# Causal mask of a diagonal score tile: two products with 128 columns of weights for eight with 32

## What is computed

```
scores = einsum('bhqd,bhkd->bhqk', q, k)           # 16 heads of 8 features, 2048 x 2048
scores = where(causal, scores, -inf)
attn   = softmax(scores / sqrt(8), axis=-1)
ctx    = einsum('bhqk,bhkd->bhqd', attn, v)
```

## Time and profile before

| | |
|---|---|
| median of 3 runs | 1156.01 us (1155.78 to 1160.44) |
| the profiled execution's own time | 1162.2 us |
| its span | 1160.4 us |
| PE busy | 1054.0 us (91%), 14718 products |
| VectorE busy | 972.7 us (84%) |
| ScalarE busy | 661.3 us (57%) |
| L1985 products | 2048, mean 222 ns |
| attention layers | about 185 to 572 and 751 to 1134 us |

### The profile page before, as it was taken

The page is one execution under the profiler, slowest core; times in us unless marked ns, Lnnn a source line. Parts: engine busy times, 40 slices in busy tenths (PEclk is TensorE's granted clock), DMA queues, the critical chain, the costliest instruction groups (busy, mean ns, idle before and its releaser), DMA issues.

```text
span 1160.4 us, 34497 instructions
## 1 busy us (share of the span) xinstructions
PE 1054.0 (91%) x14718; PEld 483.9 (42%) x14718; DVE 972.7 (84%) x2307; ACT 661.3 (57%) x852; POOL 100.6 (9%) x124
## 2 busy tenths in 40 slices
PE   4989968999999999999998857799999999999998
PEld 2545543333333333334557826333333333333446
DVE  7787579999999999988544866899999999998854
ACT  3322214566787778777523222246667777777784
POOL 1431010000000000000042252000000000000000
PEclk9999999999999999999998979799999999999999
DMA  5061052000000000000001032220000000000001
GB/s 166 2 255 72 28 163 67 3 2 3 2 2 2 3 3 3 2 3 3 2 30 46 29 91 82 74 57 3 2 3 3 2 3 2 3 2 3 3 3 38
DMA packets 29493, 36.68 MB, mean 32 GB/s; under 512 B 3694, under 2 KB 26388, under 8 KB 29084
## 3 DMA queue, kind: packets, MB, share of 16 engines
q1 hardware_dynamic: 27228, 29.22, 7.6%
q0 software_dynamic: 2112, 5.25, 1.7%
HBM read 15.29 MB, written 18.87 MB: 29 GB/s over the span
## 4 chain that ended last, share of the span: by engine, by line
PE 51%; DVE 38%; issue 5%; ACT 4%; DMA 1%; another core or an unknown queue 1%; POOL 0%; SPq 0%; DVEq 0%; ACTq 0%; POOLq 0%
DVE part_max L2174 28%; PE psum L1999 12%; PE psum L2020 11%; PE psum L1970 6%; PE psum L520 5%; PE psum L1648 2%; PE psum L1985 2%; ACT hidden L2113 2%; PE psum L2053 1%; PE psum L2026 1%; DVE xn L204 1%; PE psum L299 1%; PE psum L544 1%; PE psum L1247 1%; PE psum L1259 1%
## 5 line engine op out<-in xcount | busy, mean ns | idle before, releaser
L2174 DVE TENSOR_REDUCE part_max<-psum 128x1 f32<-128x512 f32 (+3 forms) x1120 | 675.2, 667 | 38.2 <-PE psum L2026 22.1
L2113 ACT ACTIVATE hidden<-psum 128x1024 f32<-128x1024 f32 (+3 forms) x640 | 539.0, 895 | 216.7 <-PE psum L1970 215.8
L2020 PE MATMUL psum<-k_slots,q_slots 128*32 128x512 f16 (+3 forms) x5120 | 390.7, 355 | 26.1 <-DVE part_max L2174 14.9
L1999 PE MATMUL psum<-hidden,v_aug 128*9 128x512 f32 (+3 forms) x2560 | 289.3, 528 | 0.1
L2020 PEld LDWEIGHTS psum<-k_slots,q_slots 128*32 128x32 f16 x5120 | 123.3, 95 | 283.9 <-DVE part_max L2174 200.7
L1970 PE MATMUL psum<-q_slots,k_slots 32*128 32x512 f16 (+3 forms) x1472 | 140.6, 328 | 9.3 <-ACT hidden L2113 7.5
L520 PE MATMUL psum<-parts,w_parts 128*128 128x512 f16 x384 | 91.4, 390 | 3.8 <-DVE parts L945 3.8
L2026 PE MATMUL psum<-ident_bf,later_keys 128*32 128x128 bf16 (+2 forms) x1408 | 91.2, 250 | 0.0
L1970 PEld LDWEIGHTS psum<-q_slots,k_slots 32*128 32x128 f16 x1472 | 42.2, 91 | 98.7 <-ACT hidden L2113 47.4
L1985 PE MATMUL psum<-later_keys,ident_bf 128*32 128x128 bf16 x2048 | 74.6, 222 | 3.1 <-DVE v_aug L344 1.4
L1999 PEld LDWEIGHTS psum<-hidden,v_aug 128*9 128x9 f32 x2560 | 61.5, 90 | 34.5 <-ACT hidden L2113 1.5
(11 more groups left out here) (284 smaller groups left out, 840.6 us busy)
## 6 DMA issues: line engine op xcount, KB each, us to landing
expert_regions<-k_slots SPq DMA_DIRECT2D x2, 4096.0 KB, 17.8
q_slots<-q_rows SPq DMA_DIRECT2D x8, 512.0 KB, 3.7
k_slots<-k_rows POOLq DMA_DIRECT2D x28, 128.0 KB, 4.1
q_slots<-in_L_ffn_W_dram SPq DMA_DIRECT2D x2, 1024.0 KB, 6.6
q_rows<-parts SPq DMA_DIRECT2D x6, 256.0 KB, 2.6
k_rows<-parts SPq DMA_DIRECT2D x6, 256.0 KB, 2.7
q_slots<-expert_regions SPq DMA_DIRECT2D x20, 64.0 KB, 1.8
sorted_rows<-xn SPq DMA_DIRECT2D x5, 256.0 KB, 2.3
```

The lines of the kernel that those rows point to most:

```text
L1999: last = pe.matmul(psum[VW * h:VW * h + DH + 1, O_BANK, off:CH], v_aug[:, j, G * g + h, :], probs[:, (2 * n + h // 2) % NP, h % 2, off:CH] ...
L2020: last = pe.matmul(psum[rows32(m), bank, a * w:(a + 1) * w], q_slots[:, g, qb * P + m * SLOT:qb * P + (m + 1) * SLOT], k_slots[:, G * g + ...
L2113: act.activation(probs[:, tile % NP, :, off:CH], psum[:, bank:bank + 2, off:CH], ACT.Exp, scale=scale).then_inc(exp_done, 1)
L2174: dve.tensor_reduce(part_max[:, step_no[s] % 2, h0:h0 + heads, i, kc], psum[:, bank, 0:heads * w].rearrange("p (a k) -> p a k", a=heads), ...
```

## The change

In `mask_tile` the inner loop over the four groups of 32 columns goes. In its place one product a bank writes all 128 partitions with all 128 columns of `ident_bf`. A tile's mask is then two products of the form 128*128 with 128 moving columns, where it was eight of 128*32. Values, semaphores, waits and the order of everything else stay. Nothing else in the kernel is touched; `rows32` is still used by the units.

```diff
--- before.py
+++ after.py
@@ -1981,9 +1981,8 @@
                     if pr == 0 and tile >= 2:
                         pe.wait_ge(exp_done, tile - 1)
                     for par in range(2):
-                        for m in range(COLS):
-                            last = pe.matmul(psum[rows32(m), S_BANKS + 2 * (tile % 2) + par, off:off + P],
-                                             ident_bf[:, rows32(m)], later_keys[:, :], start=(pr == 0), stop=(pr == 1))
+                        last = pe.matmul(psum[:, S_BANKS + 2 * (tile % 2) + par, off:off + P],
+                                         ident_bf[:, :], later_keys[:, :], start=(pr == 0), stop=(pr == 1))
                     if pr == 1:
                         last.then_inc(scores_done, 1)
```

## The result

The change makes the kernel slower: 1169.72 us median (1165.65 to 1172.82, 6 runs) against 1157.75 us (1155.78 to 1163.45, 6 runs). The ratio is 1.0093, interval 1.0069 to 1.0116, that is +8 to +13 us.

A forecast was written before the change was run, and what follows sets the result against it. VectorE was taken to bound the ascending half of an attention layer and PE the descending half. Terms 0 + 12.0 + 1.0 = +13.0 us gave a median of 1169.0 us, range 1161 to 1178.

The forecast's parts named there:

- Products: In a tile's mask, two wide products take 0.115 us against 0.12 for eight narrow; taken as 0.
- Price of a change of form: On PE, each switch between product forms costs 0.10 us, bounds 0.09 to 0.11.
- Count: Of 142 masks on the chain, 131 gain a change and 11 lose one: 120 x 0.10 = 12.0 us.
- A chain that gets longer can't end sooner: For masks on the chain of waits, the 12.0 us (10.8 to 13.2) was called close to a floor.
- Leak where VectorE bounds: Of 11.0 us PE time beside the chain, nearly all in VectorE-bound stretches, 1.0 us leaks for both layers.
- its sign: Test in the profile after: 185 to 385 us grows by less than 1 us, 385 to layer end by about 5 to 6.
- absorbed: Rival: in the PE-bound stretch, waits for VectorE absorb 5 of 6.5 us a layer; 1159; chance 0.10.
- full price: Rival: PE's lost time counts everywhere, 230 x 0.10 = 23 us, giving 1179; chance 0.07.
- faster: Rival: each mask product has a fixed price of 0.015 us, so fewer products save 12.8 us; 1143; chance 0.04.

The follow-up runs named there:

- experiment 5: Masks made wide only where the neighbouring PE product is already wide (32 of 256), against the kernel before: 0.9979, then 0.9984 on a second set.
- experiment 4: Exponential made for one head of two per tile, in the kernel before and the changed one: 1136.21 and 1149.00 us, 0.9812 and 0.9910 of the kernel before.
- the descending half (+6.8): Masks made wide only in the descending half of each attention layer (head groups 2 and 3), against the kernel before: 1.0058, +6.8 us.
- the ascending one (+2.1): Masks made wide only in the ascending half of each attention layer (head groups 0 and 1), against the kernel before: 1.0018, +2.1 us.
- the control with four extra products: Narrow masks kept, one extra column written by four 128*32 products ahead of mask 0 of each diagonal quad, against the kernel before: 1.0000.

## Why the prediction was right

The forecast was 1169.0 us, +13.0; measured were 1169.7 and a ratio worth +10.8. That the two times lie 0.7 us apart is partly luck: the median of the kernel before rose from 1156.0 to 1157.75 with more runs. The mechanism is as forecast. Taken by its steps:

- **Products.** Forecast 0; mask 0 to the scores went from 0.22 to 0.21 us. Right.
- **Price of a change of form.** Forecast 0.10; 0.09 to 0.12 in the rows above, and 0.21 for two in the turns of the PE-bound quads. Right.
- **Count.** This step was wrong. The text counted 13 wide neighbours by the columns of weights. L2032 has 16 columns and was taken for the narrow form, but it behaves as wide: 19 more neighbours. It stood in the trace of before: between its start at 222.45 and the narrow mask's at 222.66 lie 0.21 us, where the wide mask of experiment 5 follows in 0.12. Eleven of the 19 are on the chain, so its net count is 142 - 2 x 22 = 98 and not 120, and the term 98 x 0.105 = 10.3 us instead of 12.0.
- **A chain that gets longer can't end sooner.** Also too strong. Early in the layers the four masks of each have as many wide neighbours as others, so all 98 count behind the cut at 385 us, and the traces show 9.1 us there (5.8 less the clock's 1.4, and 4.7). Where the score block hid a wait for the exponential (experiment 4), the chain named PE while ScalarE was just as late, and a later start cost nothing. ScalarE's cover was left out of the sum; it is worth about 1 us, the 10.3 of the short exponential against the 9.1 here.
- **Leak where VectorE bounds.** Forecast 1.0 us for both layers in the stretch up to 385 us, measured 1.3 and 1.2, 2.6 in all. The cover held for the most part (28 quads at 0.21 would be 5.9 a layer), but the busy share of VectorE, 98%, promised more than it gave. The forecast named its sign as well: the first stretch was to grow by under 1 us, which failed in both layers, and the second by 5 to 6, where it grew by 4.4 and 4.7 without the clock.

The errors partly cancel, which is luck: 9.1 + 2.6 = 11.7 us in the traces against 12.0 + 1.0 = 13.0. The rivals fell one by one: "absorbed" by the descending half (+6.8), "full price" by the ascending one (+2.1), "faster" by the control with four extra products (1.0000).

## What to carry to other kernels

Look at the form of the products on either side before widening or narrowing one: here a change of form costs 0.10 us of PE, nearly as much as eight narrow products of 128 columns together (0.12), and four column groups in parallel are already as fast as one wide product. Read a product's form from the gap behind it in the timeline, since the columns of weights may mislead. A floor taken from the chain of waits holds only where no second engine is equally late; look whether the blocks on it have their shortest length.

## What the runs showed of the hardware

The fp32 transpose with 16 columns of weights is followed by a 128\*128 product in 0.12 us and by a 128\*32 one in 0.21: its form is the wide one. The bf16 transpose with 24 columns behind a 128\*128 product pays the 0.09 us on both sides, as a narrow one does. Two wide products directly behind a change of form start 65 to 67 ns apart, and behind another wide product 55 to 56, in the changed kernel. Halving the exponential's columns made the kernel 1.9% faster (0.9812), with PE's work the same. 19.1 of the 20.4 us that the two attention layers lost lie in the descending halves, so ScalarE holds them up too, though it is busy 57% of the span. And the granted clock fell to 1.2 GHz for 3.4 us near the end of the first attention layer in the changed kernel's profile (the stretch at 0.66) and in those of the kernel with wide beside wide; in the kernel before it fell only behind the layer, from 574.6 us on. What sets it off there stays open.
